# Issuing the first-half maximum rows ahead of the key stack's loads in the SyncE program

## The reference, cut to what matters

```python
x = x + attn_a(layernorm(x))   # 16 heads of width 8, causal, three heads reweighted
x = x + ffn(layernorm(x))      # 128 -> 512 -> 512 -> 512 -> 128, silu gate and two gelus
x = x + attn_b(layernorm(x))   # 16 heads of width 8, rotary, not causal
x = x + ffn(layernorm(x))
# in both attentions:
scores = einsum('bhqd,bhkd->bhqk', q, k) / sqrt(8)
out = einsum('bhqk,bhkd->bhqd', softmax(scores), v) @ Wo + bo
```

## Time and profile before

| what | value |
|---|---|
| median of 3 runs | 2515.53 us (2514.89 to 2515.76) |
| profiled execution | 2512.21 us, its span 2510.5 us |
| mean granted TensorE clock | 0.914 |
| PE busy | 2132.8 us, 85% of the span |
| DVE, ACT, POOL busy | 69%, 59%, 39% |
| DMA | 136.48 MB, mean 54 GB/s |

### The profile page before, as it was taken

How to read it: one execution, slowest core, us unless ns; L and a number is a source line. 1 busy time by engine, 2 the same in 40 slices (tenths; PEclk the granted TensorE clock), 3 DMA queues, 4 the chain that set the end, 5 groups by cost and what they waited for, 6 DMA issues and landing times. The chain is left out here.

```text
span 2510.5 us, 37314 instructions
## 1 busy us (share of the span) xinstructions
PE 2132.8 (85%) x13378; PEld 978.4 (39%) x13378; DVE 1729.4 (69%) x2590; ACT 1482.9 (59%) x2980; POOL 982.5 (39%) x1184
## 2 busy tenths in 40 slices
PE   0889999898996899999379889989998885999998
PEld 0323333233331677777112222222222211777776
DVE  5766777677670666665189899989989833667663
ACT  0265656666663556655127777777777772665655
POOL 2344555454542344554323232323323200544544
PEclk8688988889895899999659999999999986999999
DMA  6243534334331000000323423443343300000000
GB/s 172 64 99 66 114 69 93 85 79 103 66 66 20 1 1 1 1 1 1 75 51 66 104 64 66 88 89 66 67 104 67 66 15 10 8 10 14 13 10 17
DMA packets 99853, 136.48 MB, mean 54 GB/s; under 512 B 20560, under 2 KB 81488, under 8 KB 93520
## 3 DMA queue, kind: packets, MB, share of 16 engines
q1 hardware_dynamic: 99664, 134.02, 24.5%
HBM read 67.91 MB, written 55.57 MB: 49 GB/s over the span
## 5 line engine op out<-in xcount | busy, mean ns | idle before, releaser
L576 DVE TENSOR_REDUCE b_negmax<-ps_max 128x2 f32<-128x1024 f32 x512 | 611.5, 1219 | 97.5 <-PE ps_max L693 95.4
L660 ACT ACTIVATE b_prob<-ps_score 128x512 f32<-128x512 f32 x1024 | 547.7, 598 | 206.8 <-PE ps_score L679 205.6
L660 ACT ACTIVATE a_prob<-ps_score 128x512 f32<-128x512 f32 (+3 forms) x1024 | 384.5, 437 | 259.4 <-PE ps_score L679 256.8
L576 DVE TENSOR_REDUCE a_negmax<-ps_max 128x2 f32<-128x256 f32 (+3 forms) x512 | 410.9, 821 | 178.8 <-PE ps_max L697 173.6
L679 PE MATMUL ps_score<-b_stack_q,stack_k 50*128 50x512 bf16 x1024 | 263.5, 396 | 54.6 <-ACT b_prob L660 46.1
L714 PE MATMUL ps_out<-b_prob,b_v_aug 128*9 128x512 f32 x2048 | 277.7, 615 | 18.3 <-ACT b_o_raw L633 12.5
L493 POOL TENSOR_SCALAR_AFFINE_SELECT a_prob<-a_prob 128x512 f32<-128x512 f32 x256 | 162.5, 635 | 320.9 <-ACT a_prob L660 320.7
L974 PE MATMUL ps_score<-fb_h,w_hi 128*128 128x512 f32 x1024 | 251.9, 401 | 29.8 <-DVE fb_h L888 28.8
L974 PE MATMUL ps_score<-fa_h,w_hi 128*128 128x512 f32 x1024 | 251.5, 400 | 29.7 <-DVE fa_h L888 28.7
L693 PE MATMUL ps_max<-stack_k,b_stack_q 48*128 48x512 bf16 x1024 | 233.5, 396 | 40.6 <-issue 23.8
L679 PE MATMUL ps_score<-a_stack_q,stack_k 50*128 50x512 bf16 (+3 forms) x1024 | 202.2, 330 | 37.5 <-DMA a_stack_q<-a_nm_rows 30.6
(11 more groups left out here) (139 smaller groups left out, 2961.1 us busy)
## 6 DMA issues: line engine op xcount, KB each, us to landing
stack_k<-d_stack SPq DMA_DIRECT2D x64, 384.0 KB, 5.9
d_stack<-a_parts SPq DMA_DIRECT2D x64, 192.0 KB, 4.1
a_stack_q<-d_stack SPq DMA_DIRECT2D x32, 384.0 KB, 5.5
d_stack<-b_parts SPq DMA_DIRECT2D x64, 192.0 KB, 3.7
b_stack_q<-d_stack SPq DMA_DIRECT2D x32, 384.0 KB, 5.5
d_stack<-a_parts SPq DMA_DIRECT2D x64, 128.0 KB, 3.6
d_stack<-b_parts SPq DMA_DIRECT2D x64, 128.0 KB, 3.4
d_stack<-a_parts SPq DMA_DIRECT2D x64, 64.0 KB, 3.7
```

The costliest lines, as they stand in the source:

```text
L576: dve.tensor_reduce(m["negmax"][:, t, :, p], dve_banks("max", k)[:, :, 0:keys], AX.X, ALU.max, negate=True).then_inc(s["max"], 1)
L660: act.activation(m["prob"][u % PROBS][:, g, lo:S], act_bank("score", 4 * u + g)[:, 0:S - lo], ACT.Exp).then_inc(s["prob"], 1)
```

## The change

The last two pieces of SyncE's list for a step change places.

```diff
                 if on(n, 3):
                     spread_reciprocals(n - 3)
+                if on(n, 1):
+                    aug(0, n - 1)
                 if on(n, 0):
                     load(n, "stack_k", "stored_k", 1)
-                if on(n, 1):
-                    aug(0, n - 1)
```

## The result

The changed kernel is slower: 2531.45 us median of 5 runs (2528.68 to 2533.56) against 2515.53 (2512.37 to 2520.26), a ratio of 1.0062 with a 95% interval of 1.0048 to 1.0077. The distance of the medians is 15.9 us; 1.8 was forecast, and a range that ended at 2526. Measured twice more beside the kernel before, on two different chips, the ratio was 1.0037 (1.0011 to 1.0064) and 1.0034 (1.0014 to 1.0055). So the sign holds in all three comparisons; the size is 9 to 16 us by the ratios, 7 to 16 by the medians. The profiled execution of the changed kernel is one of its runs, 2531.45 us with a span of 2529.7, 19.2 more than before.

The account below looks back on a forecast made before the run. The key chain (store, landing, load, landing) was taken to set stage a's step. A gain of 7.1 us and added delay of 8.9 gave +1.8 before the clock, counted as 0: 2517.3 us from 2515.53, range 2508 to 2526.

Parts of the forecast that it names:

- What bounded the kernel: Stage a's step boundaries: rows and keys arrive almost together, keys 0.4 us earlier; the key chain of store and load sets the step.
- The gain: Stage a's 15 boundaries: scores run in PE's idle time and maxima start when keys land, saving 7.1 us in all.
- the added delay: SyncE in stage a: issuing the rows first delays key loads where the pause is short, 8.9 us over 13 steps.
- The hand-over: Stage a's boundaries: the time from the keys' landing to the start of PE's maxima, 0.1 us.
- The moved wait: SyncE's wait for the copied rows, now ahead of the key load: rows are ready in time, counted as 0.
- stage b: Its first scores wait for ACT's exponentials, not a DMA: counted as 0, bounds -1 and +3 us, 48.9 a step.
- The clock: PE's granted clock in stage a's steps: 3.6 us per lost step, as many won as lost, so 0 in the sum.
- The first rival: Delayed loads make stage a's held boundaries lose full clock: +5.4 us for one step, +12.6 for all three; chance 0.24.
- The third rival: The rows' packets hold up the keys on shared DMA engines, up to 0.4 us in 15 steps, total +7.8; chance 0.12.

Follow-up runs that it names:

- e1: The changed kernel with eight discarded matmuls over 48 rows at the head of each step of stage a: 2483.8 us, ratio 0.9871 to the kernel before.
- e2: The kernel before with eight discarded matmuls over 48 rows at the head of each step of stage a: 2478.2 us, ratio 0.9875.
- e9: The changed kernel with eight discarded matmuls a step over all 128 rows: 2478.4 us, ratio 0.9874 to the kernel before.
- e10: The kernel before with eight discarded matmuls a step over all 128 rows: 2470.8 us, ratio 0.9841.
- e12: The changed kernel with twelve discarded matmuls a step over 128 rows: 2473.5 us, ratio 0.9844 to the kernel before.
- e13: The kernel before with twelve discarded matmuls a step over 128 rows: 2475.8 us, ratio 0.9840.
- e4: The kernel before with two spare 512-byte DMAs issued ahead of the key loads in stage a, rows still behind them: 2522.0 us, ratio 1.0035.
- e3: The changed kernel with the four spreads of the reciprocals issued behind the key loads: 2500.5 us, ratio 0.9933 to the kernel before.

## Why the prediction was wrong

**What bounded the kernel: right.** Rows and keys arrived together, and the key chain set the step. The wait for the rows was replaced by one for the keys of the same 30.6 us.

**The gain and the added delay: right in mechanism and about right in size.** The hand-over took 0.1, the pair 1.5 with its gap, and the load came 1.55 behind the spreads where the pause was short. The delay summed to 8.3 us for 8.9. Forecast was +1.8 us in all before the clock, and PE's idle time in stage a grew by 1.8; that the two agree to the tenth is luck, since that idle time is 60.1 and 57.9 us in the two profiles of before and 61.9, 55.9 and 62.1 in the three of after. Where fillers kept most steps at full clock, the two orders differ at the medians by 5.6 us (e1, e2), 7.5 (e9, e10) and -2.3 (e12, e13), and the intervals of the ratios overlap in each pair. Nothing of 16 us is there.

**The moved wait and stage b: right.** SyncE issued the rows right behind the spreads, and stage b kept its 48.9 a step.

**The clock: the step that failed.** I wrote "I expect as many to be won as lost, so 0 in the sum". Three steps were lost and none won. What the term measured in the profiles was +14.3 us, PE's longer busy time in stage a. Two parts of it were off. The first is the trade at the boundaries. I expected 1.3, 1.45 and 2.1 us of idle time where the clock had held; PE's idle time ahead of the maxima there came out as these rows of after show (1.36, 1.29 and 0.95 before, in this order):

```profile
276.08 0.23 PE L693 MATMUL ps_max<-stack_k,a_stack_q 48*128 48x128 bf16 x2 [1.70 <-DMA stack_k<-d_stack]
...
321.14 0.23 PE L693 MATMUL ps_max<-stack_k,a_stack_q 48*128 48x128 bf16 x2 [2.57 <-DMA stack_k<-d_stack]
...
723.03 0.23 PE L693 MATMUL ps_max<-stack_k,a_stack_q 48*128 48x128 bf16 x2 [1.60 <-DMA stack_k<-d_stack]
```

So each was 0.2 to 0.5 longer than I had worked out, with a further 0.19 ahead of the scores, and all the steps behind them fell. At the last one the delay was smaller than I had it (0.8 for 1.0) and the load's landing longer, 6.9 us behind the first issue where it was 6.3. On the other side nothing was won: where the clock had fallen before, it fell again behind idle times as short as 1.43, 1.67 and 1.77 us, though 1.36 had held. I had taken the twelve boundaries that fell as nearer to holding than they were: the 2.2 us that I gave as their mean is that of all 14 waits of the earlier trace rows, and without the two that held it is 2.4. I had also credited the 0.35 us of the two score matmuls as time won from idleness. Whether they counted for that wasn't tried alone; in e1 eight matmuls over 48 rows in the same place left nine of 14 steps without the full clock, and the scores are over 50 rows. The second part is the price: the first two lost steps cost 3.7 and 3.6 us of busy time, as I had it, but the last one 6.3, because there the clock fell twice, near 725 and near 742 (mean 0.81).

**The rivals.** The first rival, all three held boundaries lost by the load's delay, is what happened in this pair of profiles: it was priced at +12.6 and given 0.24 with its lesser forms; the median moved by 15.9. That it was just three is partly chance, as the next profile of before had four full steps and one of the changed kernel had one; the two later comparisons, 9 us each by the ratios, would have ended within the range. e4 shows that a delay is enough to bring such a loss about, e3 that without the delay the order is a gain, and e12 and e13 that nothing else of this size is in it. The third rival, packets in front of the keys, is out as the cause: in step 8 the load landed 6.2 us after its issue and 6.3 before, and over steps 3 to 15 the mean from the first load's issue to the landing is 6.85, 6.61 and 6.86 us in the three profiles of the changed kernel against 6.67 and 6.76 in the two of before. The range failed since it weighed the boundaries as if winning and losing were alike. Most of them had already lost the clock and waited for longer than any that held; the few that held had nothing to win and, with 0.7 to 1.0 us of delay, something to lose.

**What stays open.** Why the first comparison gave 15.9 us and the later two 9 and 8.5 by the ratios. What decides, besides the length of the idle time, whether the clock falls: e3 held behind 1.48 us and fell behind 1.14, and e1 fell behind 0.4 to 0.5 where e2, with the same fillers, held behind 0.74. And the 3.7 us behind stage a, seen in one pair of profiles only.

## What to carry to other kernels

When a matrix engine waits briefly at the same place of each step, ask first behind which of these waits it still has its full clock. A reordering worth tenths of a microsecond can cost those steps several microseconds each, and the waits that are much longer win no clock back by becoming a little shorter. Where a small urgent DMA is to pass a large one, move the unurgent ones out of the large one's way in the same edit: rows first was worth +9 to +16 us with the four spreads ahead of the load, and -12 (-17 by the ratio) with them behind. Idle time that can't be removed can be filled: against the kernel before, eight discarded matmuls a step gave between 1.2 and 1.6%, in either order and over 48 rows or 128.

## What the runs showed of the hardware

The granted clock of TensorE, full at 2.4 GHz and half at 1.2, was lost, in the kernels without fillers, behind idle times as short as 1.14 us (e3) in otherwise dense work and held behind 1.48 in the same profile, so no one length parts the two; a loss cost 3.6 to 3.7 us of PE's busy time in a step of 40. Eight matmuls over 48 rows and eight over 128 rows took the same time (376 and 379 ns each); in the one profile of each in the changed order 5 and 14 of 14 steps had the full clock, in the order of before 13 and 14. The time of one kernel moves with the clock from run to run: the kernel before was seen between 2494.6 us (mean granted clock 0.921) and 2529.5 us (0.907) over the four chips, with 3 and 4 full steps in its two profiles.
